# Attention scores in a fused macaron kernel: one fp32 product, or three fp32r products of high and low parts

## The reference

```python
x = L0_attn_x
x = x + 0.5 * _L0_ffn_ref(_layernorm(x, axis=-1), L0_ffn_weight, L0_ffn_bias)
x = x + _L0_attn_ref(_layernorm(x, axis=-1), L0_attn_W)
x = x + 0.5 * _L0_ffn_ref(_layernorm(x, axis=-1), L0_ffn_weight, L0_ffn_bias)
x = x + 0.5 * _L1_ffn_ref(_layernorm(x, axis=-1), L1_ffn_Wq, L1_ffn_Wk, L1_ffn_Wv, L1_ffn_Ws, L1_ffn_Wd, L1_ffn_Wo)
x = x + _L1_attn_ref(_layernorm(x, axis=-1), L1_attn_W_in, L1_attn_conv_w, L1_attn_conv_b, L1_attn_W_x, L1_attn_W_dt, L1_attn_b_dt, L1_attn_A_log, L1_attn_D_param, L1_attn_W_out)
x = x + 0.5 * _L1_ffn_ref(_layernorm(x, axis=-1), L1_ffn_Wq, L1_ffn_Wk, L1_ffn_Wv, L1_ffn_Ws, L1_ffn_Wd, L1_ffn_Wo)
return x
```

```python
scale = DH ** (-0.5)
q = jnp.einsum('btc,hdc->bhtd', x, Wq)
k = jnp.einsum('btc,hdc->bhtd', x, Wk)
gate_v = jnp.einsum('btc,hec->bthe', x, Ws)
w, sel = jax.lax.top_k(gate_v, K)
wsig = jax.nn.sigmoid(w)
...
v = jnp.einsum('bthe,bted->bhtd', mix_v, proj_v)
scores = jnp.einsum('bhid,bhjd->bhij', q * scale, k)
probs = jax.nn.softmax(scores, axis=-1)
attn = jnp.einsum('bhij,bhjd->bihd', probs, v)
gate_o = jnp.einsum('btc,hec->bthe', x, Wd)
_, sel_o = jax.lax.top_k(gate_o, K)
```

## Time and profile before

| what | before |
|---|---|
| median of three runs | 2796.3 us (2793.99 to 2802.63) |
| profiled execution, its own time | 2803.4 us |
| its span | 2801.5 us |
| granted clock of TensorE, mean | 0.966 |
| busy: TensorE, its weight loads | 2579.3 us, 1712.1 us |
| busy: VectorE, ScalarE, GpSimd | 2187.3 us, 1855.6 us, 737.2 us |

### The profile page before, as it was taken

The page is one execution under the profiler, slowest core; times in us unless marked ns, Lnnn a source line. Parts: engine busy times, 40 slices in busy tenths (PEclk is TensorE's granted clock), DMA queues, the critical chain, the costliest instruction groups (busy, mean ns, idle before and its releaser), DMA issues.

```text
span 2801.5 us, 51283 instructions
## 1 busy us (share of the span) xinstructions
PE 2579.3 (92%) x17437; PEld 1712.1 (61%) x17437; DVE 2187.3 (78%) x3233; ACT 1855.6 (66%) x4430; POOL 737.2 (26%) x564
## 2 busy tenths in 40 slices
PE   4499999998999998999899999999999999899997
PEld 2366665665666655666565665656566665666665
DVE  5688776889889788987987889797777878775552
ACT  2256665867678576875776867687677768666563
POOL 1000000345045214512540443064144315410000
PEclk8699999999999999999999999999999999999998
DMA  3234353564565646546464654666466465545434
GB/s 134 71 114 119 97 145 97 140 174 125 144 155 146 165 112 170 152 125 163 132 171 109 171 146 138 147 167 173 112 176 172 130 159 144 161 124 149 108 80 91
DMA packets 753407, 385.77 MB, mean 138 GB/s; under 512 B 421568, under 2 KB 678656, under 8 KB 752768
## 3 DMA queue, kind: packets, MB, share of 16 engines
q1 hardware_dynamic: 749216, 380.79, 51.4%
q10 hardware_dynamic: 3936, 1.70, 0.2%
HBM read 274.91 MB, written 115.87 MB: 139 GB/s over the span
## 4 chain that ended last, share of the span: by engine, by line
PE 59%; DVE 22%; issue 9%; ACT 3%; DMA 3%; POOL 2%; SPq 1%; DVEq 0%; ACTq 0%; POOLq 0%
PE ps L723 12%; PE ps L732 11%; PE ps L745 11%; PE ps L792 7%; DVE h_ring L1223 6%; PE ps L712 6%; PE ps L798 3%; DVE h_nmax L1043 3%; PE ps L805 2%; DVE h_ring L1233 2%; PE ps L764 1%; POOL h_ring L659 1%; PE ps L832 1%; ACT h_prob L891 1%; DVE h_wide_a L1195 1%
## 5 line engine op out<-in xcount | busy, mean ns | idle before, releaser
L891 ACT ACTIVATE h_prob<-ps,h_nmax 128x512 f32<-128x512 f32 x1024 | 710.6, 696 | 141.6 <-DVE h_nmax L1043 139.6
L1043 DVE TENSOR_REDUCE h_nmax<-ps 128x2 f32<-128x1024 f32 x512 | 621.9, 1215 | 142.7 <-PE ps L723 142.4
L732 PE MATMUL ps<-ident,h_prob 128*128 128x128 f32 x4096 | 623.6, 279 | 27.0 <-DVE h_probT L1283 15.2
L732 PEld LDWEIGHTS ps<-ident,h_prob 128*128 128x128 f32 x4096 | 481.2, 144 | 197.8 <-issue 120.9
L723 PE MATMUL ps<-h_qk 64*128 64x512 f32 x2048 | 587.6, 651 | 0.9 <-ACT h_prob L891 0.8
L668 POOL TENSOR_TENSOR h_wide_c<-h_wide_c,h_ring 128x512 f32<-128x512 f32 x240 | 331.1, 1380 | 731.7 <-DVE h_ring L1233 731.7
L1011 ACT ACTIVATE h_probT<-ps 128x512 f32<-128x512 f32 x796 | 478.7, 601 | 60.8 <-PE ps L732 57.9
L745 PE MATMUL ps<-h_probT,h_v_sb 128*64 128x256 f32 x4096 | 502.7, 388 | 5.8 <-DMA h_v_sb<-v_d 3.6
L745 PEld LDWEIGHTS ps<-h_probT,h_v_sb 128*64 128x64 f32 x4096 | 273.4, 137 | 314.5 <-issue 145.2
L1223 DVE TENSOR_TENSOR_SCAN h_ring<-h_ring 128x512 f32<-128x512 f32 x256 | 397.3, 1552 | 37.6 <-POOL h_ring L659 21.3
L659 POOL TENSOR_TENSOR h_ring<-h_m_xpad,h_m_b_rows 128x512 f32<-128x512 f32 x256 | 349.7, 1376 | 259.0 <-DVE h_m_xpad L1342 250.0
(11 more groups left out here) (222 smaller groups left out, 2678.5 us busy)
## 6 DMA issues: line engine op xcount, KB each, us to landing
h_mix_diag<-mix_blocks SPq DMA_DIRECT2D x128, 512.0 KB, 3.9
v_d<-h_v_mixed SPq DMA_DIRECT2D x128, 256.0 KB, 4.3
h_v_sb<-v_d SPq DMA_DIRECT2D x128, 256.0 KB, 3.4
at_d<-h_att SPq DMA_DIRECT2D x128, 256.0 KB, 2.8
h_mo_diag<-mo_blocks SPq DMA_DIRECT2D x128, 256.0 KB, 3.4
h_att<-at_d SPq DMA_DIRECT2D x128, 256.0 KB, 3.7
h_m_b_rows<-dbl_d SPq DMA_DIRECT2D x128, 256.0 KB, 4.3
h_m_c_rows<-dbl_d SPq DMA_DIRECT2D x128, 256.0 KB, 4.3
```

Of the source, the lines that this page charges most:

```text
L732: ins = pe.transpose(ps[:, TB + v % 2, k * P:(k + 1) * P], prob[:, v % NB, k * P:(k + 1) * P], ident[:, :])
L891: act.activation(prob[:, v % NB, :], ps[:, SB + v % 4, :], ACT.Exp, bias=nmax[:, p, j, o:o + 1], accum_out=den[:, p, j, o:o + 1]).then_inc ...
L1043: dve.tensor_reduce(nmax[:, p, j, :], ps[:, SB + 2 * w % 4:SB + 2 * w % 4 + 2, :], X, ALU.max, negate=True).then_inc(sem("row_max"), 1)
```

## The change

Two fp32r tiles, `qk_hi` and `qk_lo`, stand in for the fp32 tile `qk`. ScalarE copies each `pq` and `pk` twice: to `qk_hi`, which rounds it, and to one fp32 tile `qk_raw`. VectorE subtracts the first from the second into `qk_lo` (`low_part`, two steps after the piece). `scores` then issues three products for each head, high by high, low by high and high by low, summed in PSUM, and waits for the low parts instead of ScalarE's copy. ScalarE's second copy waits until VectorE has read the previous content of `qk_raw`. `pq` goes four steps earlier and `pk` one.

To make room, `x_prep`, `x_post`, `nrm` and `nT` become one buffer `x_io`: the loads and ScalarE's copy follow one another through it, `post` loads its rows at u=20 instead of 14 and waits until the next job's gates and split are done with it. `g_rest` goes: the first choice is masked in `gates` itself. `chosen` is one tile, for the values first and for the output afterwards. The weights are split from `prob` instead of `qk`.

```diff
@@ -105,8 +105,7 @@
         ln = {"stats": sb("stats", [P, J, 6]), "mv": sb("mv", [P, J, 2]), "var_e": sb("var_e", [P, J]),
-              "rstd": sb("rstd", [P, J]), "nrm": sb("nrm", [P, J, D])}
-        nrm = ln["nrm"]
+              "rstd": sb("rstd", [P, J])}
...
@@ -240,7 +239,7 @@
             "heads": [(4 * a + 10, "att", a) for a in range(HALF)] + [(8 * p + 17, "back", p) for p in range(PAIRS)]
-            + [(8 * p - 5, "pq", p) for p in range(PAIRS)] + [(8 * p - 4, "pk", p) for p in range(PAIRS)],
+            + [(8 * p - 9, "pq", p) for p in range(PAIRS)] + [(8 * p - 5, "pk", p) for p in range(PAIRS)],
             "post": [(16 + 4 * c, "omix", c) for c in range(NCO)] + [(47, "out", 0)],
...
@@ -324,15 +323,14 @@
-            x_prep = t("x_prep", [P, J, D])
-            x_post = t("x_post", [P, J, D])
-            nT = t("nT", [P, S])
+            x_io = t("x_io", [P, J, D])
+            ln["nrm"] = nrm = x_io
+            nT = x_io[:, :, :].rearrange("p j c -> p (j c)")
...
-            g_rest = t("g_rest", [P, J, H * E])
-            chosen = t("chosen", [P, 2, J, H * E])
+            chosen = t("chosen", [P, J, H * E])
...
@@ -344,7 +342,9 @@
-            qk = t("qk", [P, 2, 2, S])
+            qk_hi = t("qk_hi", [P, 2, 2, S], F32R)
+            qk_lo = t("qk_lo", [P, 2, 2, S], F32R)
+            qk_raw = t("qk_raw", [P, S])
...
@@ -410,7 +410,7 @@
                 w_load[name] = w.rearrange("h d c -> (h d) c").rearrange("(a p) c -> p a c", p=P)
-            qk_f32 = qk[:, :, :, :].rearrange("p a b s -> p a (b s)").rearrange("p a (n c) -> p a n c", c=P)
+            qk_f32 = prob[:, :, :].rearrange("p (a b) s -> p a (b s)", a=2).rearrange("p a (n c) -> p a n c", c=P)
             att_flat = att[:, :, :, :].rearrange("p a j c -> p (a j c)")
...
@@ -576,13 +576,16 @@
                                         att2_load(n, c)
-                                if u == 14:
+                                if u == 20:
                                     if n >= 1:
                                         sp.wait_ge(sem("x_out"), 16 * n)
-                                    sp.dma_start(x_post[:, :, :], rows(x_in[n])).then_inc(sem("x_post_in"), 16)
+                                    if n + 2 < NJ:
+                                        wait_full(sp, "gate", 1, n + 2)
+                                        sp.wait_ge(sem("nT_split"), n + 3)
+                                    sp.dma_start(x_io[:, :, :], rows(x_in[n])).then_inc(sem("x_post_in"), 16)
                                 if u == AT["out", 0] + 3:
                                     wait_taken(sp, "out", 0, n)
-                                    sp.dma_start(rows(x_res[b] if kind_ == 0 else out[b]), x_post[:, :, :]
+                                    sp.dma_start(rows(x_res[b] if kind_ == 0 else out[b]), x_io[:, :, :]
                                                  ).then_inc(sem("x_out"), 16)
...
@@ -622,9 +625,12 @@
                                         sp.wait_ge(sem("x_mamba_out"), 16 * (b + 1))
-                                    if n >= 2:
-                                        sp.wait_ge(sem("normed"), n)
-                                    sp.dma_start(x_prep[:, :, :], rows(x_in[n])).then_inc(sem("x_prep_in"), 16)
+                                    if n >= 3:
+                                        sp.wait_ge(sem("x_out"), 16 * (n - 2))
+                                    else:
+                                        wait_full(sp, "gate", 1, n - 1)
+                                        sp.wait_ge(sem("nT_split"), n)
+                                    sp.dma_start(x_io[:, :, :], rows(x_in[n])).then_inc(sem("x_prep_in"), 16)
                                 for j in range(J):
...
@@ -716,12 +722,14 @@
                         if j == 0:
-                            wait_taken(pe, "pk", p, i)
+                            pe.wait_ge(sem("qk_lo"), 2 * (PAIRS * i + p + 1))
                         if w >= 2:
                             pe.wait_ge(sem("prob"), 2 * w - 2)
-                        for o in range(2):
-                            ins = pe.matmul(ps[:, SB + 2 * w % 4 + o, :], qk[o * DH:(o + 1) * DH, p % 2, 0, j * P:(j + 1) * P],
-                                            qk[o * DH:(o + 1) * DH, p % 2, 1, :], start=True, stop=True)
+                        for k_, (q_, k) in enumerate(((qk_hi, qk_hi), (qk_lo, qk_hi), (qk_hi, qk_lo))):
+                            for o in range(2):
+                                ins = pe.matmul(ps[:, SB + 2 * w % 4 + o, :],
+                                                q_[o * DH:(o + 1) * DH, p % 2, 0, j * P:(j + 1) * P],
+                                                k[o * DH:(o + 1) * DH, p % 2, 1, :], start=(k_ == 0), stop=(k_ == 2))
                         ins.then_inc(sem("score"), 1)
...
@@ -920,12 +928,12 @@
                                 act.wait_ge(sem("score"), w)
-                            ins = act.activation(qk[:, c % 2, 0 if what == "pq" else 1, :], bank, ACT.Copy)
+                            act.activation(qk_hi[:, c % 2, 0 if what == "pq" else 1, :], bank, ACT.Copy)
+                            if PAIRS * n + c >= 1 or what == "pk":
+                                act.wait_ge(sem("qk_lo"), 2 * (PAIRS * n + c) + (what == "pk"))
+                            ins = act.activation(qk_raw[:, :], bank, ACT.Copy)
                         elif what == "norm":
-                            if n >= 1:
-                                wait_full(act, "gate", 1, n - 1)
-                                act.wait_ge(sem("nT_split"), n)
-                            ins = act.activation(nT[:, :], bank, ACT.Copy)
+                            ins = act.activation(nT, bank, ACT.Copy)
                         elif what == "gate":
...
@@ -1043,6 +1051,13 @@
+                    def low_part(what, p, n):
+
+                        m = 0 if what == "pq" else 1
+                        wait_taken(dve, what, p, n)
+                        dve.tensor_tensor(qk_lo[:, p % 2, m, :], qk_raw[:, :],
+                                           qk_hi[:, p % 2, m, :].bitcast(F32), ALU.subtract).then_inc(sem("qk_lo"), 1)
+
                     def pair_done(i, p):
...
@@ -1111,14 +1126,14 @@
                         elif part == 5 and r == 0:
-                            if a == 1 and i >= 1:
+                            if a == 0 and i >= 1:
                                 dve.wait_ge(sem("mo_out"), 16 * i)
...
                             link(dve.scalar_tensor_tensor(
-                                out=g_rest[:, :, :].rearrange("p j c -> p (j c)"),
+                                out=gates[:, a, :, :].rearrange("p j c -> p (j c)"),
                                 in0=key.rearrange("p n e -> p (n e)"), scalar=NEG,
...
@@ -1287,7 +1302,12 @@
                         for kind, n, u in live(g):
-                            if kind == "prep":
+                            if kind == "heads":
+                                for p in range(PAIRS):
+                                    for what in ("pq", "pk"):
+                                        if u == AT[what, p] + 2:
+                                            low_part(what, p, n)
+                            elif kind == "prep":
                                 if u == AT["norm", 0] + 2:
```

18 lines of the change are left out of this document (9 added, 9 removed).

## The result

The changed kernel takes 2839.2 us (median of four runs, 2830.8 to 2842.3) against 2797.2 us of the kernel before beside it (2794.0 to 2802.6): 1.0143 times, with a 95% interval of 1.0115 to 1.0171, or +42 us. The forecast had +12 us as its likeliest value and 2758 to 2880 us as its range: the direction is right and the time lies inside the range, but the size is less than a third of what was measured. The profiled execution took 2842.3 us, its span is 2840.5 us, and the mean granted clock 0.955 against 0.966.

A forecast was written before the change was run, and what follows sets the result against it. TensorE was taken as first bound, VectorE in much of the rest. Path terms -47 (scores), +56 (low part) and +6 (copy) sum to +15; with the windows' -1, +12 was taken: 2808 to 2815 us, range 2758 to 2880.

The forecast's parts named there:

- moved steps, shared buffer: Moving pq and pk and sharing x_io was counted as zero, with 0 to +10 us kept for the later post load.
- TensorE's scores: Six fp32r matmuls per score step save 0.16 us on each of 512: 82 us on TensorE, 47 on the path.
- ScalarE's second copy: 256 extra copies of pq and pk at 0.48 us: +123 us on ScalarE, +6 us on the path.
- VectorE's low part: 256 subtractions at 0.65 us: +166 us on VectorE, +56 us on the path by a 34% share.
- L712's tail: Next work starts 0.17 us before L712's modelled end, 0.07 before the scores'; keeping 0.07 gives a new step of 0.90 us.
- the rival of the heads one after the other: The two heads' fp32r score matmuls do not overlap: +276 us on TensorE, about 3030 us; chance 0.05.
- The windows: 20 us windows: 43 with VectorE full lengthen (+52 us), 57 shorten (-34), 32 outside give -19; sum -1 us.
- TensorE's saving comes through: Rival: VectorE's added work hides in its existing waits; -15 to -82 us, middle -45, 2751 us; chance 0.30.
- VectorE becomes the bound: Rival: in jobs 2 to 13 VectorE's 10.4 us a job add in full; +105 us, 2901 us; chance 0.20 (+50 to +120).
- halfway: The rival of VectorE binding through the recurrence, realised only by half: +60 us, 2856 us.
- The threshold that the prediction named: VectorE's binding decides where its share passes some 90% of a job; it was 84% at 1163 us, 154/172 is 90%.
- The forecast of signs: Expected profile: score step 0.90 us, VectorE near 2350 us, TensorE waits up 30 to 60, middle jobs up to 5 us longer.

The follow-up runs named there:

- layout: The changed kernel cut to its moved steps and shared buffer: one rounded copy, fp32 scores of the high parts, no low part; 2799.8 us, ratio 1.0012.
- old_steps: The changed kernel with pq and pk back at steps 8p-5 and 8p-4; 2842.4 us, 1.0152 times the kernel before.
- pe_only: The changed kernel with the three fp32r products but only one copy and no low part (low parts are zeros); 2765.0 us, 0.9882 times the kernel before.
- no_low: The changed kernel with both ScalarE copies but no VectorE low part (low parts are zeros); 2766.8 us, 0.9888 times the kernel before.
- no_raw: The changed kernel without ScalarE's second copy; VectorE still makes 256 low parts, from a tile of zeros; 2833.2 us, 1.0138 times the kernel before.

## Why the prediction was right in kind and small in size

The mechanism held: an addition to VectorE that costs more, in the jobs with a recurrence, than TensorE saves, and a gain in the last two jobs. One sum sizes it, each term from its own pair of kernels:

| term | on the engine, forecast | on the path, forecast | measured, kernels |
|---|---|---|---|
| moved steps, shared buffer | 0 | 0 | 0 (layout); steps moved back: +3 (old_steps) |
| TensorE's scores | -82 | -47 | -35 (layout, pe_only); -32 under load |
| ScalarE's second copy | +123 | +6 | +2 (pe_only, no_low); +6 (no_raw) |
| VectorE's low part | +166 | +56 | +72 (no_low, after); +68 (pe_only, no_raw) |
| sum | | +15, taken as +12 | +39; measured whole +42 |

Of the 30 us between +12 and +42, the low part has 16 (72 in place of 56) and TensorE's saving 12 (35 in place of 47). The second copy gives 4 back. Taking +12 in place of +15 has 3, and 3 lie between the sum of the parts and the whole, within the intervals. The two large misses add; the time is inside the range because the range was wide, not because errors cancelled.

**TensorE, per step: right; on the path: too much.** The step is 0.90 us, as worked out from L712's tail, and the heads overlap, so the rival of the heads one after the other is out. The Trainium skill's page "FP8 and Floating Point Precision" (TensorE Precision Notes), read as three passes for four, gave 0.265 us a step; the trace shows 0.16. That the change between 64-row tiles and the whole array makes the difference is the forecast's reading of the tails, and no run tests it. But of the 82 us only 65 show as less busy time: with less to do and the same VectorE to wait for, TensorE had more gaps, and its clock took 10 to 18 back. Of those 65, 0.54 were on the path, close to the 57% forecast; of the 82 it is 0.43. The share of busy time was nearly right, and what the clock takes back was not in the sum. The busy time "near 500 us for the line" held: the three forms have 263, 208 and 207 us, but overlap each other, and the line as a whole is busy 510 us.

**VectorE, the work: right; the share: too small.** The forecast had 166 us of occupied queue; busy time grew by 167. The record is 0.77 us in the mean, over the 0.65 to 0.73 named, but overlaps its neighbours. What was too small is the share, 34% for a part that queues with the scans and gates, where the runs give 43%. The half low part cost 0.31 of its work, about the chain's 34%, a whole one 0.43 and two 0.50, at which point the chain has VectorE and TensorE level, 40 to 41. This fits a share of the chain that prices only the first microseconds, but with three amounts in one kernel that is a reading, not a rule.

**The windows pulled the wrong way.** The prediction settled on "+12 between them". It had said that added work can only lengthen a path beyond today's. It then let the count of full windows, -1 us, pull the sum down, by 3 us. That count took 57 windows as paid by TensorE alone, with VectorE's 10.4 us a job free there. The kernel after has 58 full windows in place of 43: the added work filled windows that were just under the limit. By its own words the chain's sum with today's shares should have been the least cost, and the measured +42 lies above it.

**The clock's part in it.** The forecast of low parts priced VectorE's queue alone. Each microsecond that TensorE waits can also cost clock behind it, as at 624 us: of low parts for 72 us, 20 are seen as longer TensorE busy time, and of double ones for 175, 56. Without these the shares are (31 - 10)/102 = 0.21 for half, (72 - 20)/167 = 0.31 for one and (175 - 56)/349 = 0.34 for two: none above the forecast's 34%. With the clock lost over all executions, 4, 19 and 51 us, they are 0.26, 0.32 and 0.36. That is arithmetic, and takes all of the lost clock as on the path. The ten executions of layout speak for that: from the one of 2794.0 us (clock 0.966) to the one of 2817.8 (0.957) the clock lost grows by 26 us and the time by 24. But no run here holds the clock fixed.

**The rivals.** TensorE's saving comes through: false for the whole change, and what pe_only and no_low show (-35 and -33 us) once the low part is out. VectorE becomes the bound (+105, halfway +60): the changed kernel, +42, stands between the forecast and halfway. The threshold that the prediction named, 90% of a job, was passed in four of the twelve jobs, and is no point at which the loss begins. Two jobs, from row maximum to row maximum (columns as above):

```profile
481.40:654.20 172.80, 161.24 (x1152) 115.30 (x1152) 158.33 (x216) 131.68 (x311) 67.19 (x48) 0.94 0.57 152
1178.50:1356.10 177.60, 164.16 (x1186) 116.97 (x1186) 152.70 (x233) 128.93 (x306) 48.78 (x35) 0.96 0.51 135
```

The first has VectorE at 92% and is 2.5 us shorter than before; the second has it at 86% and is 5.7 us longer. The Trainium skill's page "Perfetto Trace Analysis" (Identifying the Most-Contended Engine), by weight-load share, put VectorE ahead of TensorE. These runs bear that out only in part. 167 us more on VectorE cost 72 us, so it was no engine with room. But a microsecond of busy time was worth no less on TensorE, 0.54 and 0.48 when it was taken out, than on VectorE, 0.31 to 0.50 when it was added.

**Moves.** The zero stands for pq, pk and the load of the post stage. That pk follows `back`, whose taking now has a low part in front, is seen: TensorE's wait for attention rows at L718 rose from 13.2 to 20.7 us, and to 38.6 with two low parts; in no_low it is 6.9. That ties it to the low part, and the runs don't say how much of the 72 us it is.

**ScalarE.** Right: +117.5 us of busy time, 2 to 6 us of time.

**The forecast of signs.** The busy times of VectorE and ScalarE, TensorE's 89%, the score step and the shorter last jobs came as forecast. The low part's record is longer than the 0.65 to 0.73 us, and some middle jobs grew by more than the 5 us named, up to 7.3, though none by 8. Waits on TensorE for VectorE and copies were to grow by 30 to 60 us. The two lines of L740 and the one of L718 grew from 39.1 (15.2 + 13.2, and 10.7 for ScalarE's copy) to 88.8, +50. The number is in the band, but as a sign of the cost it misleads: 38 of it is the wait for ScalarE's copy, which no_low has with none of the loss.

## What to carry to other kernels

A share of the chain is a first price of a change, and not an exact one. In this kernel added work on VectorE cost about its share (0.31 against 34%) in a small amount and more in larger ones, and work taken from TensorE gave back less than its 57%. Half and twice the amount show how the price bends. Subtract in one run, add in another: two kernels, one with each term alone, settle more than the profile of both together, whose largest new wait here cost nothing. Check the granted clock in both: in these runs a TensorE that waited more also ran slower.

A second copy on an engine with slack (2 us here) may be worth more than its saving: dropping it brought the subtraction a step forward in VectorE's queue and made the release of the bank wait for it, and together they cost 73 us.

## What the runs showed of the hardware that was not expected

GpSimd isn't free beside VectorE. 256 subtractions 128x512 on GpSimd (1.46 us each by the record) lengthened VectorE's unchanged instructions by 100 us of busy time: the scan from 1.56 to 1.70 us, its product from 0.72 to 0.78, and steps of the gates from 0.73 to 0.79 and from 0.78 to 0.84. No row shows where the two engines meet; that VectorE is slower beside this work is what the rows show.

A tile of 64 rows in fp32r runs beside the one of the other 64 rows, as in fp32: six products of 512 columns in 0.90 us.

The clock takes back part of what TensorE saves. It is 0.965 with fp32 scores, 0.958 with three fp32r products and 0.931 with one, with 18 and then another 70 us of full speed lost; over all executions it is 12 and then 57. That is a seventh to a fifth of the first saving, 82 us, and a quarter or somewhat more of the second, 241.
